# A second chain of transferred sums joined into the first, and another split of the additions

## The reference, cut to what matters

```python
scores = jnp.einsum('bhqd,bhkd->bhqk', qh, kh) * scale
scores = jnp.where(mask[None, None], scores, -jnp.inf)
attn = jax.nn.softmax(scores, axis=-1)
out = jnp.einsum('bhqk,bhkd->bhqd', attn, vh)
```

## Time and profile before

| | us |
|---|---|
| median of 3 runs (lowest, highest) | 3097.92 (3094.03, 3099.81) |
| the profiled execution | 3099.21 |
| its span | 3097.6 |
| PE busy, share of the span | 2919.1, 94% |
| DVE, ACT, POOL busy | 1803.8, 1512.7, 1591.6 |
| L959, the additions on POOL, 264 of them | 1240.9 |
| L1160, the matmuls on the chains | 54.7 |
| mean granted PE clock | 0.966 |

### The profile page before, as it was taken

The page is one execution under the profiler, slowest core; times in us unless marked ns, Lnnn a source line. Parts: engine busy times, 40 slices in busy tenths (PEclk is TensorE's granted clock), DMA queues, the critical chain, the costliest instruction groups (busy, mean ns, idle before and its releaser), DMA issues. The chain is left out here.

```text
span 3097.6 us, 42919 instructions
## 1 busy us (share of the span) xinstructions
PE 2919.1 (94%) x15944; PEld 1707.3 (55%) x15944; DVE 1803.8 (58%) x3438; ACT 1512.7 (49%) x2860; POOL 1591.6 (51%) x662
## 2 busy tenths in 40 slices
PE   7979999999999999999999999996859999999996
PEld 6867555554455554555554555533645666555653
DVE  3357788875588874778865888801642333233333
ACT  2122456666566666566666566663224333443332
POOL 0000276889567899568897578897531110111110
PEclk9989899999999999999999999997979999999998
DMA  5548445558544569444578344463882110111000
GB/s 193 190 152 267 111 118 138 126 117 192 140 111 110 124 132 210 117 112 114 124 155 175 114 114 113 113 154 90 323 275 76 55 55 19 37 55 55 28 28 14
DMA packets 142342, 383.03 MB, mean 124 GB/s; under 512 B 12192, under 2 KB 29088, under 8 KB 120640
## 3 DMA queue, kind: packets, MB, share of 16 engines
q0 software_dynamic: 26512, 184.83, 24.8%
q1 hardware_dynamic: 109328, 185.30, 20.5%
q10 hardware_dynamic: 6304, 10.26, 1.0%
HBM read 122.98 MB, written 79.17 MB: 65 GB/s over the span
## 5 line engine op out<-in xcount | busy, mean ns | idle before, releaser
L1020 ACT ACTIVATE pT<-s_bank 128x512 f32<-128x512 f32 (+5 forms) x2176 | 1083.9, 579 | 678.2 <-PE s_bank L1180 507.2
L1039 DVE TENSOR_REDUCE row_max<-m_bank 128x1 f32<-128x512 f32 (+4 forms) x2240 | 1250.3, 622 | 255.9 <-PE m_bank L1133 156.3
L959 POOL TENSOR_TENSOR part_sum<-part_sum,pT 128x2048 f32<-128x2048 f32 x236 | 1113.2, 4717 | 87.8 <-ACT pT L1020 79.6
L1180 PE MATMUL s_bank<-q_sb,k_sb 104*128 104x512 f32 (+3 forms) x2176 | 845.3, 412 | 19.4 <-ACT pT L1020 14.2
L1133 PE MATMUL m_bank<-k_sb,q_sb 96*128 96x512 f32 (+4 forms) x2240 | 850.1, 411 | 8.0 <-DVE den L1066 2.8
L1133 PEld LDWEIGHTS m_bank<-k_sb,q_sb 96*128 96x128 f32 x2240 | 430.6, 196 | 221.6 <-DVE row_max L1039 149.7
L1180 PEld LDWEIGHTS s_bank<-q_sb,k_sb 104*128 104x128 f32 x2176 | 412.0, 192 | 205.5 <-ACT pT L1020 114.4
L1197 PE MATMUL o_bank<-pT,v_sb 128*32 128x512 f32 (+5 forms) x4352 | 505.2, 582 | 0.0
L1575 POOL TENSOR_TENSOR f_var_eps<-f_mean_var,eps 128x4 f32<-128x4 f32 x8 | 1.6, 201 | 567.2 <-DVE f_mean_var L1735 567.2
L959 POOL TENSOR_TENSOR part_sum<-pT 128x2048 f32<-128x2048 f32 x28 | 127.7, 4561 | 248.3 <-ACT pT L1020 204.6
L1197 PEld LDWEIGHTS o_bank<-pT,v_sb 128*32 128x32 f32 (+1 forms) x4352 | 114.1, 110 | 232.3 <-ACT pT L1020 120.9
(11 more groups left out here) (187 smaller groups left out, 3387.4 us busy)
## 6 DMA issues: line engine op xcount, KB each, us to landing
moved_sum<-pT POOLq DMA_DIRECT2D x168, 1024.0 KB, 7.1
q_sb<-qT_hi SPq DMA_DIRECT2D x64, 256.0 KB, 5.1
k_sb<-kT_hi SPq DMA_DIRECT2D x48, 256.0 KB, 7.2
x_in<-in_x SPq DMA_DIRECT2D x8, 1024.0 KB, 9.4
qT_hi<-q_hi SPq DMA_DIRECT2D x8, 1024.0 KB, 4.3
qT_lo<-q_lo SPq DMA_DIRECT2D x8, 1024.0 KB, 7.4
q_sb<-qT_lo SPq DMA_DIRECT2D x32, 256.0 KB, 4.7
aT<-o_sb ACTq DMA_DIRECT2D x32, 256.0 KB, 5.7
```

The lines of the kernel that those rows point to most:

```text
L959: pool.tensor_tensor(total, pT[:, slot(S - 1), :, q0:] if j and kt == 1 else total, pT[:, slot(S), :, q0:], ALU.add).then_inc(pool_added, 1)
L1020: act.activation(pT[0:rows, slot(S), h, q0:], s_bank[(HG * S + h) % S_RING][0:rows, q0:], ACT.Exp, scale=SCALE).then_inc(exp_done, 1)
L1039: dve.tensor_reduce(row_max[:, j % 2, r, h, c:c + 1], m_bank[p % M_BANKS][:, 0:n], AX_X, ALU.max).then_inc(unit_max, 1)
L1180: mm = pe.matmul(out[:, q0:], k_sb[0:R_END, h, at:at + P], q_sb[j % QBUFS][0:R_END, h, q0:], start=True, stop=kt < 4 * j)
```

## The change

`adder` no longer goes by a rule but by a table, `MOVES[j]`: the tiles of a first chain, those of a second one, and the step at which the second chain is accumulated into the first by a transfer of its own (`joined`, issued by `join`). Blocks 1 and 2 have one chain only, blocks 3 to 6 have two that are joined, and block 7 has two that stay apart. In block 7 the tiles from 22 on go by "matmul". `chains_left` tells how many chains the denominators read. In block 7 each addition of GpSimd is issued one step later than before (`late`), behind that step's transfer.

```diff
+Moves = namedtuple("Moves", "first second joined")
+MOVES = [Moves((), (), None), Moves((2,), (), None), Moves((2, 7), (), None), Moves((2, 7, 12), (4,), 9), Moves((2, 7, 12), (4, 9), 14),
+         Moves((2, 7, 12, 17), (4, 9, 14), 19), Moves((2, 7, 12, 17, 22), (4, 9, 14), 19),
+         Moves((2, 7, 12, 17), (4, 9, 14, 19), None)]
+LAST_BLOCK_TAIL = 22
 def adder(j, kt):
-    if kt > 4 * j or kt == KT - 1:
+    if kt > 4 * j or j == QB - 1 and kt >= LAST_BLOCK_TAIL:
         return "matmul"
-    return "transfer" if j and kt % 5 in (2, 4) and kt <= key_tiles(j) - 4 else "pool"
+    return "transfer" if kt in MOVES[j].first + MOVES[j].second else "pool"
+def chains_left(j):
+    return 0 if not j else 2 if MOVES[j].second and MOVES[j].joined is None else 1
 def chain(j, kt):
-    return sum(adder(j, k) == "transfer" for k in range(kt)) % CHAINS
+    return 1 if kt in MOVES[j].second else 0
 def moves(j, kt, c):
-    return adder(j, kt) == "transfer" and chain(j, kt) == c
+    return adder(j, kt) == "transfer" and chain(j, kt) == c or c == 0 and kt == MOVES[j].joined
 def starts_chain(j, kt):
-    return sum(adder(j, k) == "transfer" for k in range(kt)) < CHAINS
+    return kt in MOVES[j].first[:1] + MOVES[j].second[:1]
...
-        return T_VALUES * (1 + (CHAINS if j else 0) + own) + T_TURN
+        return T_VALUES * (1 + chains_left(j) + own) + T_TURN
...
+                def join(g, s):
+                    reach(pool, moved[0], 16 * (TR[0] * g + TR_BEFORE[0][s]))
+                    reach(pool, moved[1], 16 * (TR[1] * g + TR_BEFORE[1][s]))
+                    pool.dma_start(moved_sum[:, 0], moved_sum[:, 1], accum_op=ALU.add).then_inc(moved[0], 16)
...
+                late = None
                 for S, (g, s, j, kt) in enumerate(ALL_STEPS):
                     if adder(j, kt) == "transfer":
                         move(S, g, s, j, kt)
-                    if pool_adds(j, kt):
+                    if kt == MOVES[j].joined:
+                        join(g, s)
+                    if late:
+                        add(*late)
+                    late = (S, g, s, j, kt) if j == QB - 1 and pool_adds(j, kt) else None
+                    if pool_adds(j, kt) and j < QB - 1:
                         add(S, g, s, j, kt)
```

More of the change, by code:

```diff
@@ L1150, in denominators @@
                     reach(pe, pool_added, PO * g + PO_BEFORE[FIRST_STEP[j + 1]])
-                    for c in range(CHAINS) if j else ():
+                    for c in range(chains_left(j)):
                         reach(pe, moved[c], 16 * (TR[c] * g + TR_BEFORE[c][FIRST_STEP[j + 1]]))
```

## The result

| | before | after |
|---|---|---|
| median, us (lowest, highest) | 3097.92 (3094.03, 3105.87) | 3121.39 (3116.93, 3123.50) |
| the profiled execution | 3099.21 | 3116.93 |
| its span | 3097.6 | 3115.3 |
| PE, POOL busy | 2919.1, 1591.6 | 2917.7, 1657.8 |
| additions on POOL | 264, 1240.9 | 280, 1315.1 |

The time rose to 1.0071 of what it was, 95% interval 1.0054 to 1.0088: slower by 23.5 us, outside the range. The profiled execution of after is its fastest run, 17.7 us above the one of before; what follows is measured on these two, and the other 6 us are only in the medians.

The account below looks back on a forecast made before the run. TensorE was taken to bound the middle blocks, with GpSimd deciding at the handovers 6 to 7 and the end. The terms summed to 0.0 us against 3099.21, with the median 1.3 lower: 3098 us, range 3074 to 3112.

Parts of the forecast that it names:

- sets of blocks 1 to 5: Blocks 1 to 5 each lose one set of denominator matmuls on TensorE, 0.86 us each: -17.2 us in four groups.
- handover 3 to 4: Block 3's last transfer lands too late for its denominators by about 1.2 us a group: +4.8 us in four.
- handovers 6 to 7, with the clock and the set saved: Block 7's start waits about 5 us, less 0.86 saved: +4.1 a group, plus 1.5 for the clock in three groups.
- block 7's tail sets: Three more sets of denominators stand before the next group's scores: +2.6 us in each of three groups.
- block 7 behind the handover, and the end: Block 7's waits for landed transfers all go, -7.2 us; the last denominators start 4.9 us earlier, at the full clock.
- I take nothing: Blocks 1, 2, 4 and 5: GpSimd's lag is gone before the next denominators, 0 us; bound 4.7 us a group.
- The clock: Behind TensorE's wait at handover 6 to 7: 1.5 us in each of the first three groups, bounds 0 and 3.4.
- (a): Rival: the handover from block 6 to 7 costs nothing; -24.4 us, or 3074 us; chance 0.20.
- (b): Rival: the handover from block 6 to 7 costs half; about 3087 us; chance 0.13.
- (c): Rival: the clock falls at handovers 6 to 7 and the last denominators, +5.7 and +5.3 us: 3109 us; chance 0.17.
- (d): Rival: GpSimd bounds block 5 too, 4.7 us a group at most: 3117 us with nothing else changed; chance 0.05.
- The rule weighed: Skill's fit for 1024 KB transfers, 4.4 us: joins never wait, sum some 6 us lower; measured 7.6 us used instead.

Follow-up runs that it names:

- e9: The changed kernel with block 6's tile 24 going over TensorE as well: 3122.88 us, 1.0079 of the kernel before.
- e4: The changed kernel without `late`, block 7's additions issued in their own step again: 3113.53 us, 1.0044 of the kernel before.
- e1: The changed kernel with block 7 as before, so the change of blocks 1 to 6 alone: 3125.45 us, 1.0080 of the kernel before.
- e5: The changed kernel with each join issued behind the addition of its step: 3107.50 us, 1.0031 of the kernel before.
- e6: The changed kernel with block 6's two chains not joined, its added addition kept: 3122.16 us, 1.0068 of the kernel before.
- e2: The changed kernel with blocks 1 to 6 as before, so block 7's change alone: 3086.13 us, 0.9968 of the kernel before.
- e3: The changed kernel with block 6 alone as before: 3082.64 us, 0.9934 of the kernel before.
- e7: The changed kernel with blocks 2, 3 and 6 as before: 3079.21 us, 0.9934 of the kernel before.
- e8: The changed kernel with blocks 2, 3 and 6 as before and without `late`: 3075.88 us, 0.9924 of the kernel before.
- e10: The kernel of e8 with block 6's tile 24 going over TensorE as well: 3084.98 us, 0.9972 of the kernel before.

## Why the prediction was wrong

The terms of the sum beside what the two profiled executions show. A block's length is cut into the time up to the denominators of the block before it, those denominators, and the rest.

| term | predicted | measured |
|---|---|---|
| sets of blocks 1 to 5 | -17.2 | -15.5 (19 at -0.86; one ran at the lower clock, +0.7) |
| handover 2 to 3 | 0 | +3.5 |
| handover 3 to 4 | +4.8 | +8.6 (0, 3.3, 2.4, 2.9) |
| handovers 6 to 7, with the clock and the set saved | 3 x 5.6 + 4.1 = +20.9 | +30.0 (7.6, 6.4, 6.7, 9.2) - 2.6 = +27.4 |
| block 7's tail sets | +7.8 | +8.1 |
| start of the next group, ahead of them | 0 | +3.7 (0.9, -0.5, 3.3) |
| block 7 behind the handover, and the end | -7.2 - 9.1 = -16.3 | -19.0 + 0.2 = -18.8 |
| first group's block 3 | 0 | +5.8 |
| blocks 1, other rests and handovers | 0 | -4.5 + 0.9 |
| start of the attention | 0 | -2.2 |
| sum | 0.0 | +17.0 |

**The step that failed is the size of the handovers.** They were put at +25.7 us in all (4.8 and 20.9) and came to +43.2: 3.5, 8.6 and 27.4 at the three inside a group, and 3.7 at the one to the next group, which like the first had been put at nothing. What changed there was named: GpSimd is an addition and a wait later behind the join, the last transfer of the block goes out so much later, and its slot or `part_sum` holds the next block up (e9: it is the slot). In the second group it came out as worked out: the transfer was to land 10.6 to 11.3 us into block 7 and landed at 10.5, and the handover grew by 6.4 us, where 5.0 for the wait and 1.5 for the clock had been put in. The error is that this group's rows were taken for all groups and all blocks. Over all of after's L957 the landing is what it was the earlier trace rows:
```profile
DMA to landing us min/median/max: 6.9/7.6/14.1
```
but a block is held up by one particular transfer. At the handover 6 to 7 this is the one of tile 22. Counted from the start of block 7 it went out 7.6, 6.8, 6.8 and 5.1 us later than before in the four groups (6.2 forecast). It landed after 6.9, 6.9, 7.0 and 12.4 us (7.6 to 8.3 forecast; before 8.4, 8.3, 8.3 and 8.4). And it had been 0.5, 0.7, 0.7 and 0.07 us ahead of its slot's reuse. That makes the slot 5.7, 4.7, 4.8 and 9.0 us later, where 5.0 had been put in for each. So the shorter landings of three groups gave some 1.4 us back, and the long one of the fourth group was added whole:
```profile
2066.32 2.08 ACT L1044 ACTIVATE pT<-s_bank 128x512 f32<-128x512 f32 x4 [9.93 <-DMA moved_sum<-pT]
```
The slack could be read from the trace of before; I looked at GpSimd's last addition, 1.6 us ahead, and not at this.

The landing of 12.4 us comes back in other kernels. At the start of the last block SyncE issues three loads of 1024 KB for the stage behind the attention, and the transfer, which went out ahead of them before (2032.49, the loads from 2033.86), now goes out behind them, at 2053.88. After, SyncE there, and the window from that issue to the landing:
```profile
2050.17 0.94 SPq L1985 DMA_DIRECT2D a_in<-aT  x2
2051.16 0.50 SPq L1986 DMA_DIRECT2D o_x_in<-in_x  x1
```
```profile
2053.90:2066.30 12.40, 2.76 (x5) 1.13 (x5) 0.00 (x0) 2.50 (x6) 9.87 (x4) 0.57 0.99 280
```
The DMA engines are busy for a share of 0.99 in it (0.85 from issue to landing of the same transfer before). In all six kernels that issue this transfer behind the three loads (after, e1, e4, e5, e6, e9) it landed after 11.5 to 12.7 us, and in all six that issue it ahead of them (before, e2, e3, e7, e8, e10) after 7.5 to 8.4. So a later issue was not only later; it came into other traffic. No edit here takes the loads away, so that they are the cause is argued from these twelve traces.

Block 3's last transfer is the same case. It took 10.2, 9.4 and 9.1 us in groups 2 to 4, where 6.9 to 7.6 were put in; it now goes out beside the three loads of 256 KB that SyncE issues at block 4's start (924.51 to 925.77 in the second group). Over the kernels with the new block 3 it took 8.9 to 10.5 us in these groups, over those with the old one 7.0 to 8.1. And the forecast set its landing against the denominators at 927.80, while the slot was wanted at 926.2. Its denominators in the second group came, after, at 934.75, 9.9 us into block 4 (before at 927.80, 6.6 us into it). POOL, then PE:
```profile
910.16 14.33 POOL L977 TENSOR_TENSOR part_sum<-part_sum,pT 128x2048 f32<-128x2048 f32 x3
924.44 0.88 POOL L957 DMA_DIRECT2D moved_sum<-pT  x1
```
```profile
934.75 1.07 PE L1181 MATMUL m_bank<-part_sum,ones 128*32 128x512 f32 x8 [3.12 <-POOL part_sum L977]
```
The last row names the addition, but that was over at 910.16 + 14.33 = 924.49; the transfer issued at 924.44 landed at 934.7 and came last.

**The blocks in which "I take nothing".** In block 2 the transfer of tile 7 held block 3's start by 3.5 us in all, with 0.07 us left between landing and reuse. Blocks 4 and 5 absorbed their addition, as said (handovers 4 to 5 and 5 to 6 unchanged). The joins stood 33.7 us in 16 waits, 2.1 us each, where the rows gave 1.4 and 1.5 was put in.

**The clock.** Behind the stall at the handover 6 to 7 the denominators came another 1.9, 1.7 and 1.9 us later in the first three groups, where 1.5 was put in, and 0.2 in the fourth; no row gives the bound of 3.4. The first group's block 3, 5.8 us longer, is the clock too. After, 0.50 was granted in it for 10 us in which TensorE never stood:
```profile
461.60:471.90 10.30, 10.30 (x41) 5.22 (x41) 5.60 (x9) 3.69 (x8) 7.98 (x3) 0.50 0.57 119
```
In the 5.6 us ahead of it TensorE was busy for 5.12. e5 has the same stretch (that block takes 60.7 us in both), and e1, e3, e4, e6 and e9, with the same block 2 and 3, haven't (56.0). So it doesn't go with the change of blocks 2 and 3: two of the seven profiled executions that have it show this stretch. Why these two is open. From 340 us to the attention's end the granted clock was 0.50 for 48 us before, 72 after and 24 in e8, in part while TensorE stood.

**Block 7 and the end.** They gave 2.5 us more than predicted. Of the 7.2 us that ScalarE waited for landings inside block 7, 3.1 are left. The forecast for the last block was that it ends 5 us shorter; it is 0.7 longer, its handover taking 9.2 us and the rest giving 8.7. GpSimd's own work there was forecast rightly: from its first copy to its last addition it was to take 67.2 us, and it took 67.4. But the copy went out 24.6 us into the block, 9.2 later than before and not 4.1, as it waits for the late denominators. The 11.27 us of standing lie ahead of this copy (before 2.40); the forecast counted the first addition behind the copy, where `late` had put it, and so the 2.2 us that this costs (e4) are in its sum. The last denominators start 0.96 us behind the values and at the full clock, as said (before 9.29 us behind, and at half):
```profile
2139.58 2.07 PE L1221 MATMUL o_bank<-pT,v_sb 128*32 128x512 f32 x16
2142.61 1.06 PE L1181 MATMUL m_bank<-part_sum,ones 128*32 128x512 f32 x8 [0.96 <-POOL part_sum L977]
2143.49 1.90 PE L1184 MATMUL m_bank<-moved_sum,ones 128*32 128x512 f32 x16
```
**The rivals.** (a) and (b), a free or half-price handover, are refuted by the handovers' lengths and by e3: block 6's entry costs 27 to 39 us. (c) was right in its direction behind the handovers (values of 3.38 us after 4.22 us of standing) and wrong at the end. (d) had the right direction, in block 2 (3.5 us) and not in blocks 4 and 5. None of the four had the long landings and what they add at the handovers.

**The rule weighed.** The joins landed after 6.9/7.3/9.1 us (least, median, most), the other accumulating transfers after 7.6 in the median. The fit of the Trainium skill ("DMA: Bandwidth & Descriptors", the anatomy of one DMA issued by GpSimd) gives 4.4. The plain copies of the same 1024 KB do come out near it, 4.6 in the median; the accumulating ones do not. The same section says that a DMA engine waits for no semaphore and that any such wait stands on the issuing sequencer; the trace agrees, the join's 1.77 us is GpSimd's.

**Open.** Whether the loads make the landings long, which needs a kernel that issues them elsewhere. The 6 us between the differences of the medians and of the profiled executions. Where e4's 8 us and the last 4 of e5's 14 lie. The excess of e10.

## What to carry to other kernels

When work is put ahead of an asynchronous transfer, its landing is what comes later. So read from the trace how long ahead of its slot's reuse each such landing comes now, in every repetition; where that is under a microsecond, charge the whole delay. Read also what else the DMA queues carry at the place to which the transfer moves, and take the landing from a transfer that has such company, not from the median. A saving on the bounding engine (here 0.9 us a block) is quickly outweighed by an addition of 4.7 us on an engine that seems idle on average, if the next block starts by its last transfer. And an instruction moved behind another on an in-order queue inherits that one's wait.

## What the runs showed of the hardware

- Accumulating transfers of 1024 KB land after 7.6 us in the median before, after and in e8 (8.0 in e3) and after 12.7 to 14.1 at most. The long ones have their places: block 7's tile 14 took 12.0 to 13.2 us in the first three groups, before and after, where SyncE loads the next group's keys and values beside it, and 7.3 in the last group, where it loads nothing. The DMA share of those blocks is 0.89 against 0.58.
- TensorE's granted clock is 0.50 from 1685 to 1690 in after, at the start of a group, with PE busy in all 5.00 us; in the 6 us from 1676 it had been busy for 4.95, at the full clock. The denominators there came at 10.4 us, and in e4, where 0.50 was granted for 3.4 us there and not for 10.2, at 7.9: the same place loses more of the clock in one execution than in another, worth 2 to 3 us here.
- Behind 4.22 us of standing, values ran at 3.38 us; behind 0.96 us at the end, denominators ran at the full clock, 0.86 us a set.
